# Two of a relational convolution's three products moved out of its dense stage: twelve matmuls in one run at every fourth turn of the edge stage

## The reference

```python
def _mgcn_conv(x, edge_index, edge_type, rel, W_in, W_out, W_loop, b, n):
    src, dst = (edge_index[0], edge_index[1])
    e = edge_index.shape[1]
    half = e // 2
    m = x[src] * rel[edge_type]
    m = jnp.concatenate([m[:half] @ W_in, m[half:] @ W_out], 0)
    deg = jax.ops.segment_sum(jnp.ones((e,), x.dtype), dst, num_segments=n)
    norm = 1.0 / jnp.maximum(deg, 1.0)
    agg = jax.ops.segment_sum(m * norm[dst][:, None], dst, num_segments=n)
    return jnp.tanh(agg + x @ W_loop + b)
...
h = emb + res * _mgcn_conv(emb, ..., rel1, W_in1, W_out1, W_loop1, b1, num_nodes)
h = h + res * _mgcn_conv(h, ..., rel2, W_in2, W_out2, W_loop2, b2, num_nodes)
return h @ mu_w + mu_b
```

## Time and profile before

| what | us |
|---|---|
| median of three runs (lowest, highest) | 3220.51 (3218.99, 3220.9) |
| span of the profiled execution | 3183.3 |
| edge stage, layer 0 (75 to 1313) | 1238 |
| dense stage, layer 0 (1313 to 1451) | 138 |
| edge stage, layer 1 (1451 to 2693) | 1242 |
| dense stage, layer 1 (2693 to 2875) | 182 |
| expert network (2875 to 3183) | 308 |

### The profile page before, as it was taken

The page is one execution under the profiler, slowest core; times in us unless marked ns, Lnnn a source line. Parts: engine busy times, 40 slices in busy tenths (PEclk is TensorE's granted clock), DMA queues, the critical chain, the costliest instruction groups (busy, mean ns, idle before and its releaser), DMA issues. The chain is left out here.

```text
span 3183.3 us, 55393 instructions
## 1 busy us (share of the span) xinstructions
PE 2759.1 (87%) x20688; PEld 2587.3 (81%) x20688; DVE 2303.9 (72%) x3258; ACT 1865.5 (59%) x3179; POOL 1952.0 (61%) x2129
## 2 busy tenths in 40 slices
PE   4888888888888888797888888888888887997998
PEld 3888888888888888796877887878777786997998
DVE  6777777777677777896777777777777776995665
ACT  6556665555555555585555555555555554785444
POOL 6666666666666666455666666666666664892223
PEclk9999989999999999899999999999999999998999
DMA  8333333333333333353333333333333333452221
GB/s 259 119 90 89 89 89 90 89 89 90 88 89 90 90 88 90 92 164 104 90 90 90 89 90 92 88 90 90 89 89 92 88 90 98 136 158 90 69 67 64
DMA packets 162458, 312.57 MB, mean 98 GB/s; under 512 B 34061, under 2 KB 95309, under 8 KB 162229
## 3 DMA queue, kind: packets, MB, share of 16 engines
q0 software_dynamic: 79872, 218.21, 23.8%
q1 hardware_dynamic: 81120, 89.89, 8.8%
q10 hardware_dynamic: 1237, 1.41, 0.2%
HBM read 263.90 MB, written 45.48 MB: 97 GB/s over the span
## 5 line engine op out<-in xcount | busy, mean ns | idle before, releaser
L740 PE MATMUL edge_rg<-edge_rel_hi,edge_hot 128*128 128x256 f32 x6656 | 1551.7, 293 | 86.6 <-issue 63.0
L740 PE MATMUL edge_rg<-edge_rel_lo,edge_hot 128*128 128x256 f32 x4992 | 1312.3, 289 | 60.0 <-issue 58.9
L740 PEld LDWEIGHTS edge_rg<-edge_rel_hi,edge_hot 128*128 128x128 f32 x6656 | 1219.6, 197 | 143.7 <-issue 92.2
L548 ACT ACTIVATE edge_hot<-edge_typ,minus_type 128x512 fp32r<-128x512 f32 x832 | 526.8, 685 | 935.9 <-DMA dense_prev<-emb_t 383.9
L740 PEld LDWEIGHTS edge_rg<-edge_rel_lo,edge_hot 128*128 128x128 f32 x4992 | 983.1, 197 | 70.0 <-issue 68.5
L623 DVE TENSOR_TENSOR edge_m_lo<-edge_rg,edge_m_hi 128x1024 fp32r<-128x1024 f32 x416 | 509.3, 1224 | 241.3 <-ACT edge_m_hi L541 127.7
L604 DVE TENSOR_SCALAR edge_hot<-edge_typ,type_of 128x512 fp32r<-128x512 f32 x832 | 582.3, 741 | 12.4 <-ACT edge_hot L548 8.7
L753 PE MATMUL edge_small<-edge_m_hi,edge_sel 128*128 128x258 f32 x1664 | 458.1, 306 | 96.3 <-DVE edge_m_lo L623 90.7
L530 POOL DMA_INDIRECT edge_xg<-emb,src x416 | 399.0, 959 | 225.9 <-issue 96.2
L530 POOL DMA_INDIRECT work<-h,src x416 | 400.7, 963 | 221.9 <-issue 101.9
L530 POOL DMA_INDIRECT edge_xg<-h,src x416 | 400.2, 962 | 216.2 <-issue 102.8
(11 more groups left out here) (183 smaller groups left out, 3933.9 us busy)
## 6 DMA issues: line engine op xcount, KB each, us to landing
work<-emb,src POOLq DMA_INDIRECT x416
edge_xg<-emb,src POOLq DMA_INDIRECT x416
work<-h,src POOLq DMA_INDIRECT x416
edge_xg<-h,src POOLq DMA_INDIRECT x416
set_x_rows<-in_x SPq DMA_DIRECT2D x25, 256.0 KB, 3.9
emb<-set_e_rows SPq DMA_DIRECT2D x25, 256.0 KB, 2.9
emb_t<-acc SPq DMA_DIRECT2D x5, 1280.0 KB
dense_prev<-emb_t SPq DMA_DIRECT2D x25, 256.0 KB, 2.7
```

Of the source, the lines that this page charges most:

```text
L548: act.activation(hot[:, q % 2, c], typ[q % 2][:], ACT.Abs, bias=K["minus_type"][:, c:c + 1]).then_inc(distances, 1)
L740: ins = pe.matmul(rg[q % 2][:, t, :], hot[:, q % 2, c, t * P:(t + 1) * P], part[:, c, :], start=(c == 0 and part is rel_hi), stop=(c == FULL))
```

## The change

The product with `W_loop` and that of the left sums with `W_in` are made in the edge stages, one chunk of one of them every fourth turn (`PACE`): the loop products at groups 6, 10, ... 102, out of the node features that lie in the right half of `acc` until it is cleared, the left products at groups 110, 114, ... 206, out of the left sums, in place. For each, ScalarE casts the chunk (`chunk_high`) and later copies the product back from PSUM (`chunk_copy`), VectorE makes the low part, and TensorE runs twelve matmuls at the end of its turn (`side_columns`). A finished loop product is stored to DRAM (`loop_t`) and its chunk cleared. `one_window` of the group at which a product was begun waits until the product has been copied out of its bank. The layer-1 edge stage now also stores `h_t` and clears the right half. The dense stages keep the right half's twelve matmuls; they add the left product (`join`), scale by the inverse degree, which a small float32 matmul spreads over the partitions (`widen`), and add the loaded loop product (`add_loop`). In layer 0 the inverse degrees are made at the head of the stage, on a 128-partition copy that goes there and back by DMA; its TensorE stream is written out rather than looped. `mu_b` comes in by two matmuls per 128 rows in `project` (four per chunk) instead of GpSimd's `add_bias`. The diff, cut to its core:

```diff
+FIRST_LOOP = 6
+FIRST_LEFT = 110
+PACE = 4
...
+        made = small[0][:].rearrange("p (o n) -> p o n", o=DC)
...
+        def begins(g):
+            for stage, start in enumerate((FIRST_LOOP, FIRST_LEFT)):
+                if (g - start) % PACE == 0 and 0 <= (g - start) // PACE < CHUNKS:
+                    return stage * CHUNKS + (g - start) // PACE
+            return None
...
+            def side_work(g, q, i):
...
+                n = begins(g + 3)
+                if n is not None:
+                    if n == CHUNKS:
+                        act.wait_ge(added, PAIRS // 2)
+                    chunk_high(n)
+                n = begins(g)
+                if n is not None:
+                    chunk_copy(n)
...
+                n = begins(g - 3)
+                if n is not None and n < CHUNKS:
+                    clear(n)
...
-                over_groups(act, (0, later(distance)), (2, high), (0, later(one_hot)), (3, copy_sums), (0, clear_one))
+                over_groups(act, (0, later(distance)), (2, high), (0, later(one_hot)), (3, copy_sums), (0, side_work))
...
+                def side_columns(g, q, i):
+                    n = begins(g)
+                    if n is not None:
+                        pe.wait_ge(added, g // 2 - 2)
+                        for o in range(DC):
+                            chunk_product(n, o)
...
                 def one_window(g, q, i):
+                    n = begins(g + 2)
+                    if n is not None:
+                        pe.wait_ge(made_copied, n + 1)
                     pe.wait_ge(lo_done, g + 1)
...
-                over_groups(pe, (4, one_window), (2, relation_rows), (0, spread_later), (4, turn_over))
+                over_groups(pe, (4, one_window), (2, relation_rows), (0, spread_later), (4, turn_over),
+                            (0, side_columns))
...
             def linear(c, b, n, d, m):
+                pe.wait_ge(right_lo, c + 1)
+                wait_past(pe, joined, c - 1)
                 at = slice(0, width(c))
                 for o in range(DC):
                     cols = slice(o * P, (o + 1) * P)
                     for k in range(DC):
+                        ins = product(pe, lin[b][:, o, at], [v[:, 0, k, cols] for v in w],
+                                      [v[:, b, k, at] for v in parts_of], k == 0, k == DC - 1)
                 ins.then_inc(lin_done, 1)
...
+            def join(c, b, n, d, m):
+                dve.wait_ge(lin_done, c + 1)
+                wait_past(dve, h_done if first else h_lo, c + 1 - DEEP)
+                at = slice(0, width(c))
+                dve.tensor_tensor(z[:, d, :, at], lin[b][:, :, at], left(c, width(c)), ALU.add).then_inc(joined, 1)
...
-            over_chunks(pool, (0, previous_low), (4, inverse_deviation), (2, h_low), (2, add_bias), deep=DEEP)
+            over_chunks(pool, (0, right_low), (5, inverse_deviation), (3, h_low), deep=DEEP)
...
-                over_chunks(dve, (0, weights_low), (4, moments), (2, residual), (0, scaled_low), (1, combine),
-                            (6, columns_low), deep=DEEP)
+                over_chunks(dve, (0, weights_low), (0, bias_parts), (1, scale), (3, residual), (0, join),
+                            (5, moments), (1, add_loop), (7, columns_low), deep=DEEP)
...
-                over_chunks(pe, (0, linear), (1, to_rows), deep=DEEP)
+                over_chunks(pe, (0, linear), (0, widen), (4, to_rows), deep=DEEP, rolled=False)
             else:
-                over_chunks(pe, (0, linear), (4, to_columns), (2, project), deep=DEEP)
+                over_chunks(pe, (0, linear), (0, widen), (5, to_columns), (3, project), deep=DEEP)
...
-                over_chunks(act, (0, matrices_high), (2, tanh), (0, previous_high), (0, scaled_high), (2, h_high),
-                            (6, copy_columns), (4, normalize), deep=DEEP)
+                over_chunks(act, (0, matrices_high), (0, right_high), (2, tanh), (3, h_high),
+                            (7, copy_columns), (5, normalize), deep=DEEP)
```

More of the change, by code:

```diff
@@ L98, in over_chunks @@
     last = max(lag for lag, _ in stages)
-    apart = 2 if deep else 1 - -last // ring
+    apart = (2 if deep else 1 - -last // ring) if rolled else CHUNKS // unroll
     for c in range(apart * unroll):
         turn(c, c // unroll, c % unroll)
-    with eng.Fori(apart, CHUNKS // unroll) as i:
-        for q in range(unroll):
-            turn(unroll * i + q, i, q)
+    if rolled:
+        with eng.Fori(apart, CHUNKS // unroll) as i:
+            for q in range(unroll):
+                turn(unroll * i + q, i, q)
     for c in range(CHUNKS // unroll * unroll, CHUNKS + last):
@@ L427, in over_groups, with phase_edges @@
         turn(STEPS + t // GROUPS_IN_RING, t % GROUPS_IN_RING)
-def phase_edges(nc, K, layer, nodes, rel, nodes_t, matrices):
+def phase_edges(nc, K, layer, nodes, rel, nodes_t, loop_t, own, matrices, dst_tiles):
     first = layer == 0
@@ L512, in _ @@
             sp.wait_ge(matrices_in, 16 * len(matrices))
-            if first:
-                sp.wait_ge(columns_out, 16 * CHUNKS // 5)
+            for k in range(CHUNKS // 5):
+                sp.wait_ge(columns_out[k], 16)
+            sp.wait_ge(loop_out, 16 * CHUNKS)
         @block.gpsimd
@@ L693, in long @@
                 dve.wait_ge(win_added, GROUPS * WINDOWS + 1)
+                split_own(1)
+                for n in range(CHUNKS, 2 * CHUNKS):
+                    chunk_low(n)
             one_hot(0, 0, 0)
@@ L1111, in linear, with widen @@
                     for k in range(DC):
[L1112 to L1119 removed]
+                        ins = product(pe, lin[b][:, o, at], [v[:, 0, k, cols] for v in w],
+                                      [v[:, b, k, at] for v in parts_of], k == 0, k == DC - 1)
+                ins.then_inc(lin_done, 1)
+            def widen(c, b, n, d, m):
+                if first and isinstance(c, int) and c == 0:
+                    pe.wait_ge(inv_in, 16)
+                wait_past(pe, scaled, c - 1)
+                pe.matmul(inv[b][:, 0:width(c)], K["ones_r"][0:1].bitcast(F32), inv_row[:, ds(c * CHUNK, width(c))],
+                          start=True, stop=True).then_inc(inv_done, 1)
             def to_rows(c, b, n, d, m):
```

435 lines of the change are left out of this document (240 added, 195 removed).

## The result

The changed kernel takes 3330.65 us (median of four runs, 3328.23 to 3335.57) against 3220.7 us before in the same measurement: a ratio of 1.0347, with an interval from 1.0332 to 1.0362. On one more chip it was 3327.04 against 3218.58 (1.0331, from 1.0314 to 1.0348). It is slower by 3.4%, or 110 us.

A forecast was written before the change was run, and what follows sets the result against it. The prediction saw the edge stages bound by a ring of waits, no engine full, and the first dense stage by TensorE. It summed 3220.5 - 38 (first dense) + 77 (second dense) + 70 (edges) = 3329.5 us, range 3245 to 3425.

The forecast's parts named there:

- First dense stage: First dense stage: 24 of TensorE's 36 matmuls a chunk leave, 4.73 us a chunk falls to 3.1; -38 us, from -45 to -10.
- the head: Start of the first dense stage: fewer weight splits against two more DMA round trips, taken as even within 5 us.
- Second dense stage: Second dense stage: a chain closing within one turn lengthens 6.15 us a chunk to 10.9; +77 us, from +52 to +125.
- the term of the half clock: Second dense stage: one half-clock loss of 1.3 us a turn, 9.6 to 10.9 us; 13.4 if all TensorE's work is halved.
- sign that TensorE would be busy for less than half of the stage: Second dense stage: with moments 10 to 11 us apart and granted clock well under 0.9, this would show the chain.
- Edge stages: Edge stages: half of TensorE's added side-product time shows, +35 us a layer, +70 in all, ends 0 and +143.
- Rival 1: Edge stages: gathers set the pace and TensorE's idle time hides the side products; total 3260 us, chance 0.16.
- the reading of the ring: Edge stages: GpSimd's waits for TensorE and VectorE's 144.4 us for gathers weigh the same, so half shows.
- Rival 2: Edge stages show all +143 us, total 3403; far form, second dense stage also wholly at half clock, 3451; both 0.20.
- Rival 3: Second dense stage: the chain does not bind, VectorE's work gives 5.5 us a chunk; with hidden edges 3167 us, chance 0.08.
- Its second bound: Second dense stage: with edges at +35, the program is faster only from a turn under 5.5 us.
- Rival 4: Second dense stage: VectorE and GpSimd hinder each other less, but nothing changes while the chain binds; no chance given.

The follow-up runs named there:

- filler: Changed kernel with 28 more matmuls a chunk in the second dense stage, products thrown away; 3233.69 us, 1.0162 of the kernel before.
- moments first: Changed kernel with VectorE's moments moved ahead of scale, residual and join in the second dense stage; 3215.15 us, 1.0101 of the kernel before.
- the chains were cut: Changed kernel, second dense stage: VectorE's moments and columns_low ahead of join, ScalarE's copy_columns ahead of h_high; 3205.3 us, 0.9954 of before.

## Why the prediction was right in its sum, and wrong in two of its terms

The forecast was 3330 us and +109; measured were 3330.65 and +110. The agreement is partly luck: one term was too small by about 60 us and another too large by about 60.

**First dense stage.** Forecast -38 us; measured -47 between the last sum of layer 0 and the first message of layer 1 (155.1 to 108.2), just beyond the far end of -45. The turn itself was right: in the middle of the stage `residual` (line 1200) starts every 3.07 us (1347.7 to 1412.2 in 21 steps), and the forecast was 3.1. GpSimd is nearly full there:

```profile
1360.00:1410.00 50.00, 46.78 (x294) 35.54 (x295) 36.96 (x49) 40.73 (x82) 46.88 (x33) 1.00 0.83 258
```

Its two operations take 1.64 and 1.27 us rather than 1.30 each. The 2.75 us above are a mean over the transposes, which now run four chunks behind and end without `linear`. What the forecast missed lies at the head: the first `residual` starts 13.5 us after the last window sum (1334.2 to 1347.7) where it was 18.7 (1312.4 to 1331.1), and the prediction took the head as even. By the first profiles of before and after the whole stretch is 43 us shorter.

**Second dense stage.** The mechanism was right: `join`, `moments`, `inverse_deviation`, `normalize`, `to_columns`, `project`, `linear`, `join` in one turn. It stands in the waits of the changed kernel's stage (in 240 us: total, times, longest):

```profile
ACT work L1328 <- POOL dense_minus_mean L1141: 175.4, 18, 10.9
POOL dense_rstd L1134 <- DVE dense_mv L1216: 161.0, 18, 9.1
DVE dense_z L1178 <- PE dense_lin L157: 150.1, 18, 9.5
PE dense_tr L1289 <- ACT work L1328: 85.4, 18, 5.1
```

and in the timeline of one turn:

```profile
2781.46 0.69 DVE L1178 TENSOR_TENSOR dense_z<-dense_lin,acc 128x512 f32<-128x512 f32 x1 [7.98 <-PE dense_lin L157]
2782.07 0.68 DVE L1208 TENSOR_TENSOR dense_xb<-dense_xb,dense_mu 128x512 f32<-128x512 f32 x1
...
2783.45 0.41 DVE L1216 BATCH_NORM_AGGREGATE dense_mv<-dense_stats 128x2 f32<-128x6 f32 x2
...
2783.95 0.62 POOL L1134 TENSOR_TENSOR dense_rstd<-dense_mv,eps 128x2 f32<-128x2 f32 x1 [9.06 <-DVE dense_mv L1216]
...
2785.51 0.20 POOL L1141 TENSOR_TENSOR dense_minus_mean<-dense_minus_mean,dense_rstd 128x2 f32<-128x2 f32 x1 [0.16 <-POOL dense_rstd L1138]
...
2785.83 1.09 ACT L1328 ACTIVATE work<-dense_xb,dense_minus_mean,dense_rstd 128x256 f32<-128x256 f32 x2 [9.89 <-POOL dense_minus_mean L1141]
...
2787.05 1.11 PE L1289 MATMUL dense_tr<-ident,work 128*128 128x128 f32 x4 [4.58 <-ACT work L1328]
...
2795.46 0.69 DVE L1178 TENSOR_TENSOR dense_z<-dense_lin,acc 128x512 f32<-128x512 f32 x1 [7.99 <-PE dense_lin L157]
```

From `join` at 2781.46 to `join` at 2795.46 are 14.00 us. Up to the transposes at 2787.05 they are 5.59 us, where the prediction's links of before give 5.5. The rest, with its `project` and `linear`, takes 8.41 us where the prediction had 4.1 at full clock. In a turn of the filler run, at full clock, the same two stretches took 5.57 us (2814.95 to 2820.52) and 4.86 (to 2825.38). The step that failed is the term of the half clock: I took the single stretch of the earlier trace rows (1.3 us lost a turn, 10.9 us in all) and kept "all of it at half" (13.4) as an end. Here nearly every matmul of the chain ran at 1.2 GHz, granted clock 0.50, in turn after turn. Forecast +77 us, ends +52 and +125; measured +140, beyond the far end.

The stage took 324 us and not 259. Of the 65 us, the clock is about 40: half clock cost 3.4 us a turn (13.77 less the filler's 10.38) where 1.3 were taken, 19 times. The links are 15: 10.38 us at full clock and not 9.6, almost all of it in `project` and `linear` (4.86 and not 4.1). The five steps without `linear` took 25 us and not 18, and the stretch before the first moments 30.7 and not 27.7. The prediction's sign that TensorE would be busy for less than half of the stage also failed: it was busy for 154.6 of 240 us (2740 to 2980), since at half clock the same matmuls fill twice the time.

The Trainium skill, in "TensorE: Matmul & The Clock Gate", Part 1, says that the throttled clock is the default and that sustained work releases it. By that the prediction had put a turn at 13.4 us, and the stage's growth would have been some +125; the turns measured 13.77. The runs agree that in this stage a burst behind a rest starts at 0.50. A release by the work of one turn they show only at a burst's very end, if at all: TensorE was busy for all of 7.50 us from 2870.5 on and was granted 0.50.

**Edge stages.** Forecast +70 us, half of TensorE's 143; measured +13 on slow chips, and by moments first and filler +16 and +15 on the fast one. Rival 1, that the edges hide it, was true, and had 0.16. The failed step is the reading of the ring: I weighed GpSimd's waits for TensorE against VectorE's waits for gathers and called it even. A wait of the pacing engine for another is no measure of how much that other one would slow it; taking away 12 matmuls, or one gather, was. With three gathers the pace fell by 1.04 us a group; with 12 fewer matmuls by 0.13. The side run added 0.36 us a turn by count, to a TensorE that had been idle for 0.79 us of each (867 of 1000 us busy). Its busy time grew by 0.21 us a turn only (867 of 1000 at 5.99, 896 at 6.03), with the granted clock at 0.98 rather than 0.95.

**The rivals.** Rival 2 (edges in full) fell, while the far half of it, the dense stage wholly at half clock, came true. Rival 3 (chain not binding) fell: moments first took 80 us off by an order alone. Its second bound does not come out of its own sum, either: with edges at +35 a layer, faster would have needed a turn under about 4.6 us, and with +35 in all under about 6.0, not 5.5. Nothing rests on it. Rival 4 changed nothing, as said: `residual` still takes up to 1.85 us in the timeline of the second dense stage, off the chain.

**The baseline.** The prediction took the 37 us between span and runs for time around the span. They were the chip. It did no harm to a difference added to the timed median, but the sentence is wrong.

## What to carry to other kernels

In a software-pipelined stage written as lags and an order, follow each engine's stream from one turn to the next and ask for a chain that closes within one turn; its links' sum is the turn, whatever the engines' busy shares say, and a consumer of an old chunk put behind a wait for the newest one is how it closes. Work out such a chain at half of TensorE's clock if TensorE rests for a good part of it, since here it stayed slow with rests of 5.6 in 14 us, and even with rests of about 1 in 10.4 (moments first). And to learn what paces a ring of waits, look for the engine whose removal of work changes the pace; an engine that is 87% busy can still hide nearly all of 143 us.

## What the runs showed of the hardware that had not been expected

- TensorE kept to half clock through most of a stage although it was far from idle: in moments first it was busy for 144.6 of 160 us at a granted clock of 0.52 (at that clock each matmul also fills twice its time). With 28 matmuls more a chunk, in the changed kernel's order, it ran at 0.99, and the program was faster.
- Thrown-away matmuls paid: -58 us with 28 a chunk in the changed kernel's tail. With eight a chunk once the chains were cut the tail of the profiled execution was 16 us shorter (507.6 to 491.3), but by the ratios of the runs the gain is not clear of noise.
- Work added to or taken from TensorE came partly back as clock: in the edge stages its granted clock was 0.87 with 12 of the relation matmuls left out, 0.95 before, 0.98 with the side products and 1.00 with three gathers a group.
- The same program took 3182 us on one chip and 3219 to 3222 us on others. By the stages, the edge stages with their gathers account for 40 of the 43 us between two spans of the unchanged kernel; the dense and expert stages were alike within 3 us.
